# State-space layers: the input block and the scan block made one, with parts rounded by GpSimd and states carried by ScalarE

## The reference

```
u, z  = split(norm(x) @ in_proj.T)           # 2 x 256 channels
u     = silu(causal_conv4(u))
dt, B, C = split(u @ x_proj.T)               # 8, 16, 16 columns
delta = softplus(dt @ dt_proj.T + b)
h_t   = exp(delta_t * A) * h_(t-1) + delta_t * u_t * B_t     # 256 x 16 states
y_t   = (h_t * C_t).sum(states) + u_t * D
out   = (y * silu(z)) @ out_proj.T
```

## Time and profile before

| | us |
|---|---|
| median of 3 runs | 2059.18 (2055.73 to 2063.76) |
| the profiled execution | 2064.11 |
| its span | 2062.0 |
| TensorE, VectorE busy | 1849.6 (90%), 1575.5 (76%) |
| ScalarE, GpSimd busy | 1187.7 (58%), 543.4 (26%) |

### The profile page before, as it was taken

One profiled execution on the slowest core, in us unless ns is written; L12 is line 12 of the kernel. 1 busy time (PEld: TensorE's weight loads), 2 busy tenths in 40 slices (PEclk: granted clock), 3 DMA queues, 4 the chain that ended last, 5 costly groups with the idle time before them and its releaser, 6 DMA issues. The chain is left out here.

```text
span 2062.0 us, 47981 instructions
## 1 busy us (share of the span) xinstructions
PE 1849.6 (90%) x18588; PEld 976.6 (47%) x18588; DVE 1575.5 (76%) x3365; ACT 1187.7 (58%) x2331; POOL 543.4 (26%) x568
## 2 busy tenths in 40 slices
PE   6898888999799999998899978988769999999967
PEld 2344454444255555554544423444543555555454
DVE  5799966566789998993565558999668999999545
ACT  5666623222278887885322266665343888888815
POOL 2699930000200000000100027999230000000022
PEclk9799999999799999998799988999886999999968
DMA  4333400411312322211031114443022233332200
GB/s 157 100 124 123 138 11 0 83 49 33 109 25 54 54 55 53 51 27 22 1 83 51 31 31 122 130 123 118 1 62 60 49 57 58 59 58 42 31 5 21
DMA packets 68271, 126.88 MB, mean 62 GB/s; under 512 B 20919, under 2 KB 30676, under 8 KB 66572
## 3 DMA queue, kind: packets, MB, share of 16 engines
q1 hardware_dynamic: 67628, 123.27, 24.1%
q10 hardware_dynamic: 416, 0.54, 0.1%
HBM read 105.15 MB, written 16.84 MB: 59 GB/s over the span
## 5 line engine op out<-in xcount | busy, mean ns | idle before, releaser
L1711 ACT ACTIVATE a_probs<-a_ps_k 128x512 f32<-128x512 f32 (+3 forms) x1280 | 598.7, 546 | 225.1 <-PE a_ps_k L1625 130.0
L1607 PE MATMUL a_ps_q<-a_k_op,a_q_op 84*32 84x512 bf16 (+7 forms) x5120 | 537.5, 367 | 23.0 <-DMA a_k_op<-a_k_parts 9.6
L1771 DVE TENSOR_REDUCE a_maxes<-a_ps_q 128x1 f32<-128x512 f32 x768 | 504.2, 686 | 67.7 <-PE a_ps_q L1607 65.0
L1621 PE MATMUL a_ps_k<-a_q_op,a_k_op 87*32 87x512 bf16 (+7 forms) x5120 | 519.0, 353 | 3.4 <-issue 1.0
L1643 PE MATMUL a_ps_o<-a_probs,a_vh 128*32 128x512 f32 (+3 forms) x2752 | 319.9, 509 | 0.8 <-ACT a_probs L1711 0.8
L1607 PEld LDWEIGHTS a_ps_q<-a_k_op,a_q_op 72*32 72x32 bf16 (+1 forms) x5120 | 187.9, 97 | 170.8 <-DVE a_maxes L1771 68.9
L1768 DVE CUSTOM_DVE_ANT_0 a_ps_q<-a_ps_q,all_c_mask_q 128x128 f32<-128x128 f32 (+3 forms) x512 | 248.1, 496 | 4.9 <-PE a_ps_q L1607 3.7
L1621 PEld LDWEIGHTS a_ps_k<-a_q_op,a_k_op 75*32 75x32 bf16 (+1 forms) x5120 | 186.1, 96 | 134.6 <-ACT a_probs L1711 83.2
L1042 ACT ACTIVATE e_silu<-e_psg,all_me_b 128x512 f32<-128x512 f32 x128 | 87.7, 687 | 229.1 <-PE e_psg L974 229.0
L1851 POOL CAST a_max_parts<-a_neg_max 128x16 bf16<-128x16 f32 x32 | 6.3, 196 | 751.4 <-DVE a_neg_max L1776 751.4
L1125 DVE SCALAR_TENSOR_TENSOR e_mid<-e_psv,all_me_b,e_silu 128x512 f32<-128x512 f32 x128 | 95.7, 749 | 129.2 <-PE e_psv L976 125.3
(11 more groups left out here) (283 smaller groups left out, 2560.7 us busy)
## 6 DMA issues: line engine op xcount, KB each, us to landing
m0sc_c_rows<-m_bc_rows SPq DMA_DIRECT2D x32, 512.0 KB
e_w_rows<-e_comb SPq DMA_DIRECT2D x64, 256.0 KB, 3.3
m1sc_c_rows<-m_bc_rows SPq DMA_DIRECT2D x32, 512.0 KB
a_q_op<-a_q_parts SPq DMA_DIRECT2D x30, 288.0 KB
a_k_op<-a_k_parts SPq DMA_DIRECT2D x30, 288.0 KB
a_outputs<-a_o_sb SPq DMA_DIRECT2D x480, 18.0 KB
m0sc_b_rows<-m_bc_rows SPq DMA_DIRECT2D x32, 256.0 KB
m1sc_b_rows<-m_bc_rows SPq DMA_DIRECT2D x32, 256.0 KB
```

The source lines that it names most:

```text
L1607: last = pe.matmul(ps_q[32 * r:32 * r + 32, use % QB, 0:width], q_op[h % SLOT][0:NR, part(t, r)], k_op[h % SLOT][0:NR, kc * CH:kc * CH + w ...
L1621: last = pe.matmul(ps_k[32 * r:32 * r + 32, b % KB, 0:width], k_op[h % SLOT][:, part(j, r)], q_op[h % SLOT][:, c * CH + first:c * CH + fir ...
L1711: act.activation(probs[:, n % PSLOT, 0:width], ps_k[:, b % KB, 0:width], ACT.Exp).then_inc(exp_done, 1)
L1771: dve.tensor_reduce(found, bank, AX.X, ALU.max).then_inc(q_read, 1)
```

## The change

The two blocks become one, `mamba_state`, with all semaphores of both and shared memory: PSUM and SBUF of the input part and of the scan part overlap, and waits guard the reuse.

- The banks of the last products are written out by hand. The last xd product comes after two dt products, TensorE then turns b, makes dt for chunks 1 and 2, spreads the row of B for step 0, makes dt for chunk 3, and goes on to the turning of du and the scan's products.
- The last chunk of xd is copied by VectorE. VectorE makes du of chunks 0 and 1, the drive of step 0, du of chunk 2, the scans of step 0, and du of chunk 3 after them.
- GpSimd makes all three parts of xd (two casts, two subtractions). ScalarE's two roundings go.
- ScalarE copies the carries, in `carry_over`.
- SyncE issues the rows of steps 0 and 1 before it stores the last chunk; one semaphore per half of the tokens tells that rows are stored.

The diff, cut to its core (semaphores, names and the unchanged bodies that only move are left out):

```diff
+        c_rows = [m.sb(f"c_rows{s}", [P, SCT]) for s in range(2)]
+        b_rows = [m.sb(f"b_rows{s}", [P, CH]) for s in range(2)]
...
-        items += [("dt", c, h) for c in range(2) for h in range(NH2)]
-        items += [("xd", NC - 1, 0)]
-        items += [("dt", c, h) for c in range(2, NC) for h in range(NH2)]
+        TAIL = len(items)
+        items += [("dt", 0, 0), ("dt", 0, 1), ("xd", NC - 1, 0)]
+        items += [("dt", c, h) for c in range(1, NC) for h in range(NH2)]
+        bank_of = [k % RING for k in range(TAIL)] + [0, 1, 6, 2, 3, 4, 5, 6, 7]
...
+            for k in range(TAIL + 3):
+                make(k)
+            turn_b()
+            for k in range(TAIL + 3, TAIL + 7):
+                make(k)
+            pe.wait_ge(g.late.loaded, g.late.full)
+            pe.wait_ge(delta_ready, NH2)
+            rows(0)
+            for k in range(TAIL + 7, len(items)):
+                make(k)
+            turn_du(0)
+            products(0)
+            turn_du(1)
+            rows(1)
+            products(1)
+            pe.wait_ge(delta_ready, NH2 * NC)
+            pe.wait_ge(du_copied, 2)
+            skip(0)
+            for q in range(STEPS):
+                if q and q + 1 < STEPS:
+                    rows(q + 1)
+                    products(q + 1)
+                if q % NS == 0 and q:
+                    pe.wait_ge(gated, NH2 * (q // NS))
+                    skip(q // NS)
+                sum_states(q)
...
-                act.activation(parts[:, 1, c % 2, :], rest[:, c % 2, :], ACT.Copy).then_inc(split_1, 1)
...
-                    act.activation(parts[:, 0, c % 2, :], xd[:, chunk(c)], ACT.Copy).then_inc(split_0, 1)
...
+            for c in range(NC):
+                softplus(c)
...
+            def carry_over(q, h):
+                if q >= 0 and q // NS + 1 < NSC:
+                    act.wait_ge(scanned, NH2 * q + h + 1)
+                    act.activation(carry[:, h, q % NS:q % NS + 1], state[half(q, h)][:, SCT - 1:SCT], ACT.Copy).then_inc(carried, 1)
+            act.wait_ge(delta_ready, NH2 * NC)
+            for q in range(STEPS):
+                exps(q, 0)
+                if q == 0:
+                    act.wait_ge(b_copied, 1)
+                    diagonals(0)
+                exps(q, 1)
+                carry_over(q - 1, 0)
+                act.wait_ge(part_ready, q + 1)
+                if q:
+                    act.wait_ge(scanned, NH2 * q)
+                act.activation(drive[:, 1, MADE:SCT], part[q % 2][:, :], ACT.Copy).then_inc(part_placed, 1)
+                carry_over(q - 1, 1)
+                if q + 1 < STEPS:
+                    diagonals(q + 1)
...
+            dve.wait_ge(made, product_made("xd", NC - 1))
+            dve.tensor_copy(xd[:, chunk(NC - 1)], bank("xd", NC - 1)[0:XDBL, :]).then_inc(xd_ready, 1)
...
+            times_u(0)
+            times_u(1)
+            copy_turned(0)
+            dve.wait_ge(cleared, 1)
+            dve.wait_ge(gate_ready, NH2 * NC)
+            make_drive(0)
+            times_u(2)
+            scans(0)
+            copy_turned(1)
+            times_u(3)
...
+                pool.tensor_copy(parts[:, 0, c % 2, :], xd[:, chunk(c)]).then_inc(split_0, 1)
+                pool.wait_ge(split_0, c + 1)
+                pool.tensor_tensor(rest[:, c % 2, :], xd[:, chunk(c)], parts[:, 0, c % 2, :], ALU.subtract).then_inc(rest_ready, 1)
+                pool.wait_ge(rest_ready, c + 1)
+                pool.tensor_copy(parts[:, 1, c % 2, :], rest[:, c % 2, :]).then_inc(split_1, 1)
...
-                        pool.tensor_copy(carry[:, h, q % NS:q % NS + 1], state[half(q, h)][:, SCT - 1:SCT]).then_inc(carried, 1)
...
+                if c == NC - 1:
+                    sp.wait_ge(made, product_made("gate", NC - 1, 1))
+                    sp.wait_ge(conv, tap(NC - 1, CONV - 2, 1))
+                    load_rows(0)
+                    load_rows(1)
```

More of the change, by code:

```diff
@@ L284, in product_made, with early_chunk, time, half @@
             return items.index((what, c, h)) + 1
-        def early(k):
+        def early_chunk(k):
             return k * SCT // CH
+        def time(q, first=0, last=SCT):
+            return slice(q // NS * SCT + first, q // NS * SCT + last)
+        def half(q, h):
+            return (NH2 * q + h) % 3
         @block.tensor
@@ L312, in _ @@
[L312 to L334, removed]
@@ new lines, in rows @@
+            def rows(q):
+                if q % NS == 0:
+                    for s in range(2):
+                        pe.wait_ge(stacked[s], 16 * SPL * (q // NS + 1))
+                if q:
+                    pe.wait_ge(scanned, NH2 * (q - 1) + 1)
+                for b in range(NB):
+                    last = pe.matmul(drive[:, 0, chunk(b)], g["sel"][:, q % NS, :], bc3[:, time(q, b * CH, (b + 1) * CH)],
+                                     start=True, stop=True)
+                last.then_inc(rows_spread, 1)
@@ new lines, in products, with skip @@
+            def products(q):
+                pe.wait_ge(diag_ready, q + 1)
+                if q % NS == 0:
+                    pe.wait_ge(du_copied, q // NS + 1)
+                if q:
+                    pe.wait_ge(scanned, NH2 * q)
+                for j in range(TPC):
+                    last = pe.matmul(drive[:, 1, tile(j)], du_T[:, q // NS, j, :], diag_b[q % 2][:, j, :], start=True, stop=True)
+                last.then_inc(product_ready, 1)
+            def skip(k):
+                for h in range(NH2):
+                    for b in range(NB):
+                        pe.matmul(psy[:, h, chunk(b)], diag_d[:, h, :], u[:, h, time(NS * k, b * CH, (b + 1) * CH)],
+                                  start=True, stop=False, skip_group_check=True)
@@ new lines, in sum_states @@
+            def sum_states(q):
+                for h in range(NH2):
+                    pe.wait_ge(read_ready, NH2 * q + h + 1)
+                    for b in range(NB):
+                        last = pe.matmul(psy[:, h, chunk(b)], g["ident"][:, :], read[h][:, chunk(b)],
+                                         start=False, stop=q % NS == NS - 1, skip_group_check=True)
+                    last.then_inc(summed, 1)
+            pe.wait_ge(w.loaded, w.full)
+            for k in range(TAIL + 3):
+                make(k)
@@ L365, in _ @@
                                        ACT.Copy).then_inc(raw_copied, 1)
[L366 to L370, removed]
+                if 2 <= s < NC + 1:
                     c = s - 2
@@ L422, in _, with times_u @@
                                                      ALU.mult, ALU.add).then_inc(conv, 1)
[L423 to L429 removed]
+            def times_u(c):
```

325 lines of the change are left out of this document (148 added, 177 removed).

## The result

| | before | after |
|---|---|---|
| median, 20 runs each | 2061.91 | 2058.11 |
| ratio of after to before | | 0.9975, interval 0.9966 to 0.9985 |
| span of the profiled execution | 2062.0 | 2057.2 |
| TensorE, VectorE busy | 1849.6, 1575.5 | 1837.2, 1579.1 |
| ScalarE, GpSimd busy | 1187.7, 543.4 | 1185.0, 554.8 |

The change makes the kernel 0.25% faster: 0.0025 x 2061.9 = 5.2 us, with an interval from 3.1 to 7.0. The two medians lie 3.8 us apart. The forecast was a gain of 7.9 us. Its 2051.3 us was worked out against a kernel before of 2059.18; in these runs the same kernel took 2061.91, so 2.7 us of the distance between 2051.3 and 2058.11 are the baseline's.

What follows compares the result with a forecast made beforehand. GpSimd was taken to pace the scan's first half, TensorE the input block's end. Carries 5.1 plus head 2.8 gave 7.9 us; 2064.1 less 7.9 is 2056.2, shifted by -4.9 to 2051.3; range 2042 to 2062.

Steps and rivals of the forecast that it cites:

- Part 1, the carries: Scan's first half: carries moved to ScalarE cut the step from 6.10 to 5.91 us, 5.1 us for both layers.
- Part 2, the splitting: Input block: GpSimd's extra casts lengthen the last convolution by 0.9 us, to 46.3, still before silu at 46.75; cost 0.
- Part 3, the head: Start of both layers under the new order: step 2 scans earlier by 0.7 us in m0, 2.1 in m1.
- D: Moment the last dt product leaves TensorE in a layer's head; predicted at 63.3 us in m0, 1236.7 in m1.
- step 2 at D + 21: Scan's start: TensorE's queue of skip and sums delays the first scan of step 2 to 21 us after D.
- the sign that was named for it: Before drive 2: an idle VectorE whose wait TensorE's row spreading ends, with skip and sums right before it.
- The same sum there ... D = 1236.7: Head of m1: 2.1 us at half clock, rest of eight dt and spreading at full, last four mostly half, 3.0.
- rival B: Head: TensorE keeps full clock from x product to D; gains 8.4 and 6.0, with carries 19.5 us, 2039.7; chance 0.25.
- C: Head: skip and first sums at 1.2 GHz, m1's dt work at half clock; 8.7 us slower, 2067.9; chance 0.13.
- The product of du beside a read: VectorE's last du product beside a GpSimd read may cost 0.9 us more, hidden under TensorE's lateness.
- S (splitting hurts): Input block: convolutions wait out whole GpSimd operations, silu 1.2 us late per layer; gain 5.5, 2053.7; chance 0.07.
- E (the carries don't pay): Scan: ScalarE's copies come late and VectorE waits as before; gain only 2.8 us, 2056.4; chance 0.03.

Runs made afterwards that it cites:

- split_only: Kernel before, with only the splitting changed: GpSimd makes all three parts of xd. Ratio to before 0.9993 (0.9978 to 1.0008).
- carry_back: Kernel after, with the carry copies moved back from ScalarE to GpSimd. Ratio to before 0.9995 (0.9982 to 1.0008).
- dt_full: Kernel after, with dt products over all 128 rows, xd's tile and the weights padded with zeros. Ratio to before 0.9928 (0.9908 to 0.9947).
- carry_only: Kernel before, with only the carry copies moved from GpSimd to ScalarE. Ratio to before 0.9972 (0.9959 to 0.9985), 5.8 us faster.
- dt_wide: Kernel after, with dt products over 40 rows of xd instead of 8, weights padded with zeros. Ratio to before 0.9954 (0.9939 to 0.9968).
- full_both: Kernel after, with 128-row dt products, late du products before step 0's scans and half the skip moved earlier. Ratio to before 0.9897 (0.9874 to 0.9921).
- carry_full: Kernel before, two blocks and old order, with carries on ScalarE and dt products over 128 rows. Ratio to before 0.9911 (0.9888 to 0.9934).

## Why the prediction was right or wrong

**Part 1, the carries: right.** Predicted 5.1 us, a step of 5.91; measured 5.91 and, alone, 5.8 us. ScalarE's copies took 0.19 us each and nobody waited for them.

**Part 2, the splitting: right in sum, not in the working.** The working made the last convolution 0.9 us longer by a fourth GpSimd instruction, 7.7 us, ending at 46.3. It ended at 46.54, but only because it began at 39.96 instead of 38.65; it took 6.58 us, no longer than before (6.77), so the match is luck. It was GpSimd that took longer beside it: casts of 1.15 and 0.95 us against 0.60 for one by itself, subtractions of 1.48 against 1.15. Silu started at 48.06, 1.5 us behind the convolution, once the gate's copy was done. split_only shows no cost.

**Part 3, the head: here it failed, and this is the 2.7 us that are missing.** The way after D was right: the first scan at D + 4.5 (measured 4.0 in both layers), step 2 at D + 21 (21.1 and 19.8), with TensorE's queue late. In m0 the sign that was named for it showed, an idle VectorE before drive 2 that the row spreading ends; in m1 VectorE had no idle time there, and the spreading had ended 0.7 us before drive 2. The step that failed is D in m1: "The same sum there ... D = 1236.7" took over the mixture of clocks from the row of before. That D is 49.4 us after the layer's start; it came at 54.5, 5.0 later. Of these, 2.9 are the eight dt instructions with the spreading behind them, which were taken mostly at full clock and ran at 1.2 GHz throughout (7.19 us for the eight), 0.8 are the last four (3.78 instead of 3.0), and 1.3 lie ahead of the turn's end. There the x product took 3.04 us, and the recorded 1228.6 for the turn's end is itself about 0.6 early: silu ends at 1225.11 before, and the same way as in m0 (47.89 to 52.0) leads to 1229.2. Step 2 of m1 should have come 70.4 us after the layer's start (1257.7 less 1187.3) and came at 74.2, 3.8 late. In m0 step 2 was predicted at 84.3 and came at 83.2, which is partly luck: the eight dt instructions took 4.90 us instead of 6.9, and silu started 1.3 us later than taken. Sum of the head: 1.8 gained in m0, 1.7 lost in m1, 0.1 in place of 2.8; carry_back says the same with 0.9995. Why the clock fell where it did in an execution stays open; that it cost D its time is shown by dt_full, where D in m1 came 47.0 us after the start, as rival B has it (1234.3 less 1187.3).

The clock had its place among the rivals, but not this one. B has it full from the x product to D. C does name m1's dt work at half clock, D = 1239.9, but only together with a skip and sums at 1.2 GHz; in m1 the dt work ran at half clock and the skip then at full (3.60 us).

So the gain was real and of the side forecast, inside the range, but 5.2 us instead of 7.9; within 0.5%, to which 0.64 was given. What I missed is that a clock read from one profiled execution is not a property of the order of work, and that the base of the sum, D of before in m1 (48.2), moves as well: 47.5 to 51.6 in the three kernels with two blocks and 8-row dt products.

**The product of du beside a read** was taken at 0.9 us more; it took 3.02 instead of 1.22, 1.8 more. Its row shows how: it starts at 71.72, the read ends at 73.66, and the product ends 1.1 us after that, about its own length. GpSimd's next part, which meets the product, takes 2.25 instead of 1.27. That is what the Trainium skill, page "SBUF — State Buffer", section "Who interferes with whom", says: the loser stands for the other's whole instruction. The trace agrees, and my reading of 0.9 came from instructions half as long and GpSimd instructions of at most 1.6 us, where the read takes 2.36. "That lies under TensorE's lateness" held in m0, where 1.21 us of waiting were left; in m1 VectorE had no wait left.

**Rivals.** S (splitting hurts) is excluded by the place of silu in the traces of split_only and after, more than by the time. E (the carries don't pay) is excluded by carry_only, whose step fell to 5.91 us in both layers. B did not happen by itself. dt_full makes its clock happen: step 2 came at 80.3 in m0 and 67.9 us after the start in m1, gains of 4.7 and 4.6, where B had 8.4 and 6.0. With the 5.1 of the carries that is 14.5 us, and the ratio of 0.9928 says 0.0072 x 2062.5 = 15 (interval 11 to 19), where B had 19.5.

## What to carry to other kernels

Before two blocks are merged to fill a gap, count what stands in the one in-order queue between the first use and the second step: here the skip and the sums, 7.2 us of TensorE in m1 and 8.3 in m0, took back 1.5 and 3.9 of the 6.0 us that the end of the barrier gave. A copy of 0.2 us on the engine that sets the pace was worth more than the whole new head, and the next engine's time tells beforehand how much of it comes back. Where TensorE is the bound and a product uses few rows, look at the granted clock of that stretch over several executions; padding the product with zeros may cost nothing.

## What the runs showed of the hardware

I had not expected the granted clock to differ with the form of the product. With TensorE busy throughout by the profile, it was at 0.50 to 0.72 in the stretches around the dt products over 8 rows and over 40 rows in the kernel after and dt_wide. Over 128 rows, with the same count of instructions, the same 512 columns and the same data beside the zeros, it was 1.00 in all dt instructions of dt_full, full_both and carry_full. The time went with it: 7.19 us for eight instructions at 1.2 GHz, 3.70 at 2.4. The x product between the dt products took 1.91 us in all six of those heads, and 1.91 to 3.63 in the others. A dt product over 8 rows did not have the low clock each time: the first four of a head in the new order ran at 0.94 to 1.00. Clearing a tile of 2048 columns took GpSimd 1.8 us and, like the wider weights, cost nothing that shows in m1, where silu starts as long after the layer's start as in the kernel after. What in the wider product keeps the clock up was not tried further.
